# A two-layer gated cross-attention kernel on one core: turns of the second attention reordered, norms and slots' rows by ScalarE, routing with one division, filler products in waits

## The reference

```python
x = x + tanh(g_xattn[0]) * attn0(norm(x), ctx)    # 16 heads of 16
x = x + tanh(g_ffn[0])   * ffn0(norm(x))          # 8 experts, each for every token
x = x + tanh(g_xattn[1]) * attn1(norm(x), ctx)    # one head of 256, mask
x = x + tanh(g_ffn[1])   * ffn1(norm(x))          # 8 experts, top-1, capacity 256
```

## Time and profile before

| what | value |
|---|---|
| median of 3 runs | 764.35 us (763.16 to 766.68) |
| the profiled execution's own time | 764.7 us |
| its span, first to last instruction | 762.9 us |
| TensorE matmuls busy | 646.4 us, 85% |
| VectorE busy | 521.0 us, 68% |
| ScalarE busy | 331.2 us, 43% |
| GpSimd busy | 229.1 us, 30% |
| mean granted clock of TensorE | 0.921 |

### The profile page before, as it was taken

The page is one execution under the profiler, slowest core; times in us unless marked ns, Lnnn a source line. Parts: engine busy times, 40 slices in busy tenths (PEclk is TensorE's granted clock), DMA queues, the critical chain, the costliest instruction groups (busy, mean ns, idle before and its releaser), DMA issues.

```text
span 762.9 us, 12648 instructions
## 1 busy us (share of the span) xinstructions
PE 646.4 (85%) x4564; PEld 546.7 (72%) x4564; DVE 521.0 (68%) x1362; ACT 331.2 (43%) x530; POOL 229.1 (30%) x155
## 2 busy tenths in 40 slices
PE   5978598899899899999799889999966931799995
PEld 4656366787678778778688777898855821799995
DVE  6877987677877866866776647479458883466662
ACT  4434155355356456456355325152523321455641
POOL 2444624566532212221014010010031242255542
PEclk9879779899999999999999999999989955799998
DMA  7303303335442242333243424434221141964700
GB/s 225 121 15 127 125 1 139 125 135 211 180 166 83 85 165 84 137 113 125 83 165 113 162 87 152 132 124 146 83 69 43 61 161 43 318 210 153 242 20 26
DMA packets 43463, 94.51 MB, mean 124 GB/s; under 512 B 3519, under 2 KB 24383, under 8 KB 42384
## 3 DMA queue, kind: packets, MB, share of 16 engines
q1 hardware_dynamic: 41344, 87.62, 33.6%
q0 software_dynamic: 2064, 6.16, 2.3%
HBM read 72.94 MB, written 21.04 MB: 123 GB/s over the span
## 4 chain that ended last, share of the span: by engine, by line
PE 65%; DVE 24%; issue 5%; ACT 2%; DMA 1%; POOL 1%; DVEq 0%; SPq 0%; ACTq 0%; POOLq 0%
PE psum L1591 43%; PE psum L2097 6%; PE psum L1668 2%; PE psum L1698 2%; PE psum L1628 2%; PE psum L1662 2%; DVE work L1063 1%; DVE scratch L266 1%; DVE x_all L1079 1%; PE psum L1635 1%; PE psum L1647 1%; DVE work L951 1%; PE psum L1962 1%; PE psum L1893 1%; PE psum L1945 1%
## 5 line engine op out<-in xcount | busy, mean ns | idle before, releaser
L1591 PE MATMUL psum<-arena 128*128 128x256 f32 (+1 forms) x2544 | 446.0, 334 | 33.8 <-DVE x_all L1079 15.6
L1591 PEld LDWEIGHTS psum<-arena 128*128 128x128 f32 x2544 | 384.5, 199 | 78.4 <-DVE x_all L1079 14.8
L2135 POOL TENSOR_TENSOR diag<-neg_ident,work 128x1024 fp32r<-128x1024 f32 x32 | 60.9, 1904 | 249.3 <-DVE work L1010 242.5
L1063 DVE TENSOR_TENSOR work<-work,psum 128x512 f32<-128x512 f32 x64 | 43.9, 686 | 62.1 <-PE psum L1591 57.3
L625 ACT ACTIVATE arena<-work 128x512 fp32r<-128x512 f32 x64 | 40.3, 630 | 90.7 <-DVE work L1063 78.7
L1079 DVE SCALAR_TENSOR_TENSOR x_all<-psum,w_exp,x_all 128x256 f32<-128x256 f32 x128 | 55.9, 479 | 27.7 <-PE psum L1591 26.9
L618 ACT ACTIVATE work<-psum 128x512 f32<-128x512 f32 x64 | 38.2, 597 | 56.8 <-PE psum L1591 56.3
L1068 DVE TENSOR_TENSOR arena<-work,arena 128x512 fp32r<-128x512 f32 x64 | 51.8, 810 | 8.7 <-ACT arena L625 8.2
L2218 POOL TENSOR_TENSOR arena<-work,arena 128x1024 fp32r<-128x1024 f32 x4 | 9.5, 2370 | 151.1 <-ACT arena L641 151.1
L1010 DVE TENSOR_REDUCE work<-psum 128x8 f32<-128x1024 f32 x32 | 39.0, 1220 | 15.7 <-PE psum L1647 15.6
L593 ACT ACTIVATE work<-psum 128x1024 f32<-128x1024 f32 x32 | 32.8, 1026 | 35.4 <-PE psum L1668 32.3
(11 more groups left out here) (194 smaller groups left out, 844.8 us busy)
## 6 DMA issues: line engine op xcount, KB each, us to landing
arena<-kept SPq DMA_DIRECT2D x24, 1024.0 KB, 5.6
work<-in_w SPq DMA_DIRECT2D x16, 1024.0 KB
kept<-arena SPq DMA_DIRECT2D x8, 1536.0 KB, 6.1
arena<-kept SPq DMA_DIRECT2D x24, 512.0 KB, 4.8
work<-in_w SPq DMA_DIRECT2D x8, 768.0 KB, 7.8
slots<-fill POOLq DMA_DIRECT2D x1, 2080.0 KB
work<-in_ctxT SPq DMA_DIRECT2D x8, 256.0 KB, 3.0
work<-in_ctxT SPq DMA_DIRECT2D x4, 512.0 KB, 5.2
```

The lines of the kernel that those rows point to most:

```text
L1063: dve.tensor_tensor(gu[i % 2], gu[i % 2], ps[:, UP, :], ALU.mult).then_inc(hm, 1)
L1591: mm = pe.matmul(dst, left(i, k), right(j, k), start=(n == 0), stop=(n == 3 * K2 - 1))
L2135: pool.tensor_tensor(diag, neg_ident[:, :].rearrange("p (o q) -> p o q", o=1).to_broadcast([P, 8, P]), mx[u % 2].rearrange("p (h o) -> p h ...
```

## The change

Ten edits, in the order of the code:

1. The table of constants has token numbers for all 16 sequences, so that the counter `tokn` and `row_numbers` go; `x_all`'s number column is written once at the start.
2. `expert_weights` leaves out the division of the fallback weights and the clips, and the last division and the gate are one step.
3. `normalise_a` and `normalise_b` move from VectorE to ScalarE (scale and bias from columns); VectorE makes the bias (minus mean times reciprocal root) in one more small step behind each root.
4. The value bias, gated once at the start, is added to the rows of `x_all` by GpSimd (`value_bias`, 16 additions of 128x256); ScalarE copies v out of PSUM (`v1_evict`) in place of `v1_add`.
5. The turns have a new order on all engines: `xa_transpose` and `k1_project` of the next group come a turn earlier, `scores1` comes before `xb_transpose`, `mask_and_max` before `xb_low`.
6. `keep_warm(n)`: TensorE does n products of the identity with the mask tile into bank 0, which nothing reads: 11 in turn (3, 2), 35 in turn (None, 3) and 44 behind it.
7. The split of the first expert's weights moves from GpSimd to VectorE (`first_split`); its second half waits until all rows have landed.
8. The slots are loaded in three pieces: two, two and twelve tiles.
9. `slots_norm` moves to ScalarE, behind the fourth hidden tile; only the first rows stay with VectorE.
10. The very last down products write their second tile to another bank with a semaphore of their own, and `scatter` waits for each of its two tiles by itself.

```diff
             def expert_weights(g):
-                divide_by_sum(7)
                 seq(dve.tensor_tensor(r[7], r[7], over_e(rs[1]), ALU.mult))
                 seq(dve.tensor_tensor(rt[4], rt[4], rt[7], ALU.add))
-                divide_by_sum(4)
+                seq(dve.tensor_reduce(rs[2], r[4], AX.X, ALU.add))
+                seq(dve.reciprocal(rs[2], rs[2]))
...
-                dve.tensor_scalar(w_exp[g % 2], r[4], tgate[:, 2:3], None, ALU.mult).then_inc(s_wexp, 1)
+                dve.scalar_tensor_tensor(w_exp[g % 2], r[4], tgate[:, 2:3], over_e(rs[2]), ALU.mult, ALU.mult
+                                         ).then_inc(s_wexp, 1)
```

The order of VectorE in the last experts and its turns:

```diff
             h_low(29, 0)
-            root_b()
             accumulate(28, 0)
-            normalise_b(0)
+            root_b(0)
             h_mult(29, 1)
-            v1_add(1)
             h_low(29, 1)
             accumulate(28, 1)
-            row_numbers(0)
+            xb_low(0)
             h_mult(30, 0)
-            xb_low(0)
...
             def turn3(ga, gb):
+                more = ga is not None and ga + 1 < G
+                if more:
+                    stats_a(ga + 1, 0)
+                    moments_a(ga + 1, 0)
+                    root_a(ga + 1, 1)
                 attention_gates(gb)
                 add_attention(gb)
                 moments_b(gb)
                 root_b(gb)
+                if ga is not None:
+                    mask_and_max(ga)
                 xb_low(gb)
+                if ga is None:
+                    first_split(0, w4_l1.sem)
                 pick_expert(gb)
                 slot_and_gate(gb)
                 pick_place(gb)
+                if more:
+                    xa_low(ga + 1)
+            xa_low(2)
             turn3(2, 1)
```

ScalarE:

```diff
+            def normalise_b(g):
+                act.wait_ge(sb_ok, g + 1)
...
+                for t in range(g * GB, (g + 1) * GB):
+                    act.activation(xn_b[t % GB], x_all[:, t, 0:D], ACT.Identity, bias=x_all[:, t, D + 1:D + 2],
+                                   scale=x_all[:, t, D:D + 1]).then_inc(nb, 1)
...
             silu(29, 1)
+            v1_evict(1)
             h_high(29, 1)
+            normalise_b(0)
+            xb_high(0)
...
                 probs_copy(gb)
                 if ga is None:
                     act.wait_ge(a1, 2 * G)
                     split(0, 0, 0)
+                    split(0, 0, 1)
                 else:
-                    xa_high(ga)
-                    k1_evict(ga)
                     q1_evict(ga)
+                    if more:
+                        normalise_a(ga + 1)
+                    v1_evict(ga)
+                normalise_b(gb)
                 xb_high(gb)
...
+                        if more and f == 3:
+                            act.wait_ge(s_xs[1 + i], 16)
+                            slots_norm(*nxt)
```

TensorE:

```diff
+            def keep_warm(n):
+                for _ in range(n):
+                    pe.matmul(ps[:, 0, :], ident_b[:, :], hide[:, 0:1, :].to_broadcast([P, 4, P]), start=True, stop=True,
+                              skip_group_check=True)
+
             def turn3(ga, gb):
+                more, last = ga is not None and ga + 1 < G, ga is None
                 probs_transpose(gb)
-                if ga is not None:
-                    xa_transpose(ga)
+                if last:
+                    keep_warm(2)
                 attend(gb)
-                if ga is not None:
-                    k1_project(ga)
+                if last:
+                    keep_warm(22)
+                else:
+                    q1_project(ga)
                     v1_project(ga)
-                    q1_project(ga)
+                    scores1(ga)
                 xb_transpose(gb)
-                if ga is not None:
-                    scores1(ga)
+                if more:
+                    xa_transpose(ga + 1)
+                else:
+                    keep_warm(5)
                 logits1(gb)
+                if not more:
+                    keep_warm(2)
                 logits1_transpose(gb)
+                if more:
+                    k1_project(ga + 1)
+                else:
+                    keep_warm(4)
                 places(gb)
+            xa_transpose(2)
+            k1_project(2)
             turn3(2, 1)
             turn3(3, 2)
             turn3(None, 3)
+            keep_warm(44)
```

GpSimd:

```diff
+            def value_bias(g):
+                pool.wait_ge(s_bo, 2)
+                for t in range(g * GB, (g + 1) * GB):
+                    pool.wait_ge(na, t + 1)
+                    pool.tensor_tensor(x_all[:, t, 0:D], x_all[:, t, 0:D], bv1r, ALU.add).then_inc(xv, 1)
+
             ctx_low(0)
+            value_bias(0)
+            value_bias(1)
+            ctx_low(1)
+            value_bias(2)
             pool.wait_ge(s_disp, 16)
-            for g in range(1, G):
-                ctx_low(g)
-                if g >= 2:
-                    dispatch(g - 2)
-            dispatch(G - 2)
-            split_w1(0, 0)
-            dispatch(G - 1)
+            ctx_low(2)
+            dispatch(0)
+            value_bias(3)
+            ctx_low(3)
+            dispatch(1)
+            dispatch(2)
+            dispatch(3)
...
             def scatter(g, i):
-                pool.wait_ge(y4.sem, y4.now(g, i + 1))
-                pool.wait_ge(ds4.sem, ds4.now(g, i + 1))
                 pool.wait_ge(idx4.sem, idx4.now(g, i + 1))
                 alone(pool)
-                for j in range(2):
+                for j, rows in enumerate((ds4, y4)):
+                    pool.wait_ge(rows.sem, rows.now(g, i + 1))
+                    alone(pool)
```

More of the change, by code:

```diff
@@ L335, in block_kernel @@
         oh1, loc1, dest = sem("onehot_ready"), sem("places_ready"), sem("rows_ready")
-        s_xs = [sem("first_slots_loaded"), sem("other_slots_loaded")]
+        s_xs = [sem(f"{n}_slots_loaded") for n in ("first", "second", "other")]
         s_raw4 = [sem(f"expert1_weights_loaded{i}") for i in range(2)]
@@ L717, in _ @@
                     ctx3_high(0)
+                    normalise_a(0)
                 if runs(fb):
@@ L807, in _ @@
             h_high(26, 0)
+            v1_evict(0)
             silu(26, 1)
@@ L812, in _ @@
             silu(27, 0)
+            normalise_a(1)
             h_high(27, 0)
@@ L862, in turn3 @@
                 gate_exp(gb)
+                if more:
+                    xa_high(ga + 1)
+                if more:
+                    k1_evict(ga + 1)
+            xa_high(2)
+            k1_evict(2)
             turn3(2, 1)
@@ L880, in hidden, with slots_norm @@
                 act.activation(h4[i][0][:, f, :], ps[:, f % 4, 0:CAP], ACT.Relu).then_inc(h1_hi.sem, 1)
+            def slots_norm(g, i):
+                for j in range(2):
+                    row = xs[:, bass.ds(4 * g + 2 * i + j, 1), :].rearrange("p a c -> p (a c)") if not isinstance(g, int) \
+                        else xs[:, 4 * g + 2 * i + j, :]
+                    act.wait_ge(xd_t.sem, xd_t.now(g, 1) if i else xd_t.before(g, 2))
+                    act.activation(xd[j], row[:, 0:D], ACT.Identity, bias=row[:, D + 1:D + 2], scale=row[:, D:D + 1]
+                                   ).then_inc(xd_ok.sem, 1)
             def turn(g, last):
@@ L1380, in xb_low @@
                                       ).then_inc(nb_lo, 1)
-            top, rank, gate, row, place, own = (r3s[i] for i in range(6))
+            top, rank, gate, row, place = (r3s[i] for i in range(5))
             def over8(col):
@@ L1417, in pick_place @@
                 step(dve.scalar_tensor_tensor(row, place, float(CAP), row, ALU.is_lt, ALU.mult))
-                dve.tensor_tensor(tok_idx[:, g * GB:(g + 1) * GB], row, tokn[:, GB:2 * GB], ALU.add).then_inc(dest, 1)
+                dve.tensor_tensor(tok_idx[:, g * GB:(g + 1) * GB], row, cst[:, C_OWN + g * GB:C_OWN + (g + 1) * GB], ALU.add
+                                  ).then_inc(dest, 1)
                 if g + 1 < G:
-                    dve.wait_ge(dest, g + 1)
+                    step(dve.tensor_reduce(counted[:, :], oh_b[:, :, :].rearrange("p b e -> p e b"), AX.X, ALU.add))
                     step(dve.tensor_tensor(ones_before[:, :], ones_before[:, :], counted[:, :], ALU.add))
-                    step(dve.tensor_scalar(tokn[:, :], tokn[:, :], float(GT), None, ALU.add))
             h_mult(25, 0)
@@ L1478, in _ @@
             h_mult(30, 1)
-            normalise_a(2)
             h_low(30, 1)
@@ L1494, in _, with first_split @@
             mask_and_max(1)
+            def first_split(a, done):
+                dve.wait_ge(w4_hi.sem, w4_hi.now(0, a + 1))
+                dve.tensor_tensor(w4[0][1][:, a, :], raw4[0][:, a, :], w4[0][0][:, a, :], ALU.subtract).then_inc(done, 1)
             def turn3(ga, gb):
-                attention_gates(gb)
-                if ga is not None:
-                    xa_low(ga)
-                add_attention(gb)
-                moments_b(gb)
-                root_b()
-                normalise_b(gb)
```

(14 more changed lines are left out.)

155 lines of the change are left out of this document (74 added, 81 removed).

## The result

The changed kernel takes 740.32 us, the median of four runs (736.42 to 743.43), against 763.75 us of before (761.9 to 766.68, four runs): a ratio of 0.9687, 95% interval 0.9631 to 0.9743. The prediction said 742, 734 to 753, faster with 0.95. The profiled execution took 743.43 us with a span of 741.6; that of before 764.7 with 762.9.

The account below looks back on a forecast made before the run. TensorE was taken as the bound in the first FFN and expert stage, with waits in the second attention's turns between. The terms sum to -22.8 us, from 764.7 to 741.9, said as 742, range 734 to 753.

Parts of the forecast that it names:

- Routing, -5.2: `expert_weights`: five dependent VectorE steps for eleven shorten TensorE's wait before four accumulations by 1.3 us each, -5.2 us.
- Start and overlap, +0.8: Start and last FFN experts: extra bias product costs 0.3 us, later `xb_transpose(0)` makes the overlap net +0.5 us.
- The turns, -12.5: Second attention's turns: (2,1) -2.3 us, (3,2) -1.7, last turn -8.5, from new order, fillers and moved work.
- clock part, 3.7: Last turn: filler products keep the clock at its upper level, so products, attention and transposes save 3.7 us.
- lock part of 4.2: Last turn: `split_w1` leaves GpSimd, so the 4.2 us that VectorE stood at L266 goes.
- Dispatch, -1.2: Last group's indirect transfers: VectorE's split waits until rows have landed, so one transfer's delay of 1.14 us goes.
- Slots and first expert, -2.9: After dispatch: smaller first load, quicker transposes and first products at the upper clock (1.75 us kept of 2.5), -2.9 us.
- The end, -1.8: Last down products: first row tile leaves 2.9 us earlier, second transfer issued near 755.4 for 757.17, -1.8 us.
- B: First two turns: new ScalarE and GpSimd queues eat their gain; -14 us, 750 (748 to 755), chance 0.20.
- C: Fillers don't hold the clock in the last turn and behind it; -6 us, 758 or so, chance 0.06.
- D: ScalarE's added rows and evictions, 28 us, set the pace; slower, 770 if all on the path, chance 0.02.
- E: More than forecast in GpSimd's additions, first expert, overlap and turns; -28 us, 736 and less (to 730), chance 0.08.

Follow-up runs that it names:

- the holding back: Changed kernel with 54 fillers, second expert's weights issued behind the first piece of slots, and later loads issued only once these weights have landed: ratio 0.969, median 737.17 us.

## Why the prediction was right, and where not

**Routing, -5.2.** Right in mechanism and in the four waits (-5.3), too small in effect: with the clock's falls it was -7.1. This term, with the next, hides the failure below: of the 3.4 us that the stretch between the releases brought beyond the forecast, it has 1.9 and the reordering 1.5.

**Start and overlap, +0.8.** Sign wrong. The kernel with two divisions, which differs from before in all but this routing edit, has 422.99 us between the releases, before 423.99: the reordering gave -1.0 in the FFN's overlap where I had +0.5. The wait of 0.93 at 525 went and `xb_transpose(0)` was late by 1.37, both as said; what I had not counted is that a wait of 0.74 at 532.85 went too, and the wait ahead of group 1's scores, 2.42 us before (at 555.68) and 1.39 after, probably since VectorE has fewer steps there (not tried apart). The sign rests on one execution of each kernel.

**The turns, -12.5: -11.3.** Turn (3,2), between its row numbers, -1.7 as said; the last turn -7.5 for -8.5. Its clock part, 3.7, was measured as 3.7, its lock part of 4.2 as 4.9 (with the clock lost behind it 5.7). What is missing is in part ScalarE's rows, which take 2.06 to 2.08 us for the four where I had 1.8, in each turn. Of the last turn's missing 1.0 they are 0.3; the rest I can't assign. A fall of the clock at 575, worth 1.0, stood in turn (2,1), which came out near its forecast (-2.1 for -2.3) all the same. The lock beside `value_bias(3)`, 1.4, was measured as 1.45.

**Dispatch, -1.2: -1.3**, and +1.2 when undone.

**Slots and first expert, -2.9: +0.5.** This step failed, at the sentence "of which I keep 1.75, because the second expert's weights ... may land later than the quicker products want them". The first load did come quicker (2.81 us to the first rows, where I took 3.2). But splitting the load put two issues ahead of the weights: their split could start only 12.27 us after the load of slots where that of before could at 10.7, and in ScalarE's queue this split stands ahead of six hidden tiles. It was the bound; fillers could not help (16.71 without, 16.86 with). And "44 fillers 9.6 in a wait of 12" was taken as enough to hold the clock, which fell after the 2.25 us that they left. Two of the prediction's own signs failed here: the clock was not 1.00 throughout, and the first hidden block took 10.1 us and not 6.1 to 7.

**The end, -1.8: -1.8**, also when undone.

Of the rivals, B, C and D did not come; of E, the overlap came and the first expert did not. The version that is best by its stretches, with the weights right behind the first piece of slots and 54 fillers, has 738.36 us (with the holding back 737.17); by totals it can't be told from the changed kernel, by stretches it is 3 us better from the load of the slots on.

## What to carry to other kernels

Before you pay for a faster engine or a higher clock, follow each in-order queue to its next wait for a transfer: here ScalarE's split of the next weights stood before six tiles' copies, and nearly all of the clock's gain went into that wait until one load was issued a place earlier. Compare runs between events, not by their totals: the last stretch repeated to 0.1 us where the start alone scattered by nearly 7. A wait on TensorE can cost more than its length; count what the clock does behind it.

## What the runs showed of the hardware

Waits of TensorE that grew from 1.3 to 1.6 us to 2.5 to 2.9, four times, went with 7.1 us and not 4.75: the granted clock fell to 0.50 at two more places, and the other 2.4 us lie in the pieces with these falls. Behind the 44 fillers TensorE idled 2.25 us and the clock fell; with 54 fillers it fell some 3.4 us later, after the idle time behind the transposes, and with that filled too not at all. Small VectorE steps beside GpSimd operations on two SBUF inputs last as long as the GpSimd operation (0.64 to 0.68 beside 0.70; 5.03 beside 4.51), and GpSimd's issue of an indirect transfer waits likewise for a VectorE operation on two SBUF inputs (2.14 for 0.97). A load of two pieces of 1 MB was there 3.5 us earlier when one transfer of 0.26 MB stood ahead of it and not two, more than the bytes explain; with 0.52 MB ahead in a single transfer it wasn't late either, and in one run the order with two was 1.3 to 2.1 us better than in the seven others.
